# x1 kept in the output tensor, and the batch norm's results added to it by accumulating transfers

## The reference

```python
h = jnp.maximum(_layernorm(x, axis=-1), 0.0)
x = x + _L0_gnn_ref(h, adj, adj, Wq, Wk, Wv, Wo)      # 16-head attention with adj + adj as its bias
h = jnp.maximum(_layernorm(x, axis=-1), 0.0)
x = x + _L1_gnn_ref(h, adj, router_w, router_b, expert_w, bn_gamma, bn_beta)
...
scores = x.mean(axis=1) @ router_w + router_b
top1 = jnp.argmax(scores, axis=-1)
support = jnp.einsum('bnh,bhk->bnk', x, expert_w[top1])
out = jnp.einsum('bnm,bmk->bnk', adj, support)
# mean and variance of out over the rows of each expert's batches
y = (out - mean[top1]) * rsqrt(var[top1] + 1e-5) * bn_gamma[top1] + bn_beta[top1]
return relu(y)
```

## Time and profile before

| | us |
|---|---|
| median of 3 runs | 1561.91 (1559.69 to 1562.31) |
| the profiled execution | 1559.98 |
| its span | 1557.9 |
| PE busy in the span | 1480.9 (95%) |
| DVE busy | 1137.4 (73%) |
| ACT busy | 999.9 (64%) |
| POOL busy | 444.7 (29%) |

### The profile page before, as it was taken

The page is one execution under the profiler, slowest core; times in us unless marked ns, Lnnn a source line. Parts: engine busy times, 40 slices in busy tenths (PEclk is TensorE's granted clock), DMA queues, the critical chain, the costliest instruction groups (busy, mean ns, idle before and its releaser), DMA issues. The chain is left out here.

```text
span 1557.9 us, 39084 instructions
## 1 busy us (share of the span) xinstructions
PE 1480.9 (95%) x11474; PEld 1264.9 (81%) x11475; DVE 1137.4 (73%) x2641; ACT 999.9 (64%) x3145; POOL 444.7 (29%) x529
## 2 busy tenths in 40 slices
PE   7999999999999999999999999999969999998885
PEld 6888888888888888888888888888757777777775
DVE  4777777777777777777777777777676667676685
ACT  4667666766676677666666766676644454453495
POOL 0223222322223222222232222222223343443200
PEclk9999999999999999999999999999879999999997
DMA  5965556666655566665555666654524332220798
GB/s 180 254 145 142 125 125 144 150 151 152 144 131 125 128 148 147 155 148 145 126 125 135 148 150 151 149 139 112 136 89 135 123 124 87 67 68 14 268 406 327
DMA packets 142135, 230.37 MB, mean 148 GB/s; under 512 B 17666, under 2 KB 34050, under 8 KB 142082
## 3 DMA queue, kind: packets, MB, share of 16 engines
q1 hardware_dynamic: 133634, 212.95, 52.7%
q10 hardware_dynamic: 8448, 16.78, 2.8%
HBM read 89.15 MB, written 39.85 MB: 83 GB/s over the span
## 5 line engine op out<-in xcount | busy, mean ns | idle before, releaser
L268 POOL TENSOR_TENSOR prob<-prob,norm 128x512 f32<-128x512 f32 x256 | 266.3, 1040 | 789.3 <-DVE norm L372 789.3
L301 ACT ACTIVATE prob<-logits,neg_max 128x128 f32<-128x128 f32 x1024 | 398.1, 394 | 69.7 <-DVE neg_max L361 69.6
L43 PE MATMUL bank<-hT_hi,w_hi 128*128 128x256 f32 x1024 | 303.1, 296 | 2.5 <-DVE hT_lo L405 2.2
L43 PE MATMUL bank<-hT_lo,w_hi 128*128 128x256 f32 x1024 | 290.7, 284 | 0.0
L43 PE MATMUL bank<-hT_hi,w_lo 128*128 128x256 f32 x1024 | 290.6, 284 | 0.0
L356 DVE SCALAR_TENSOR_TENSOR logits<-scores_ps,adj 128x512 f32<-128x512 f32 x256 | 176.7, 690 | 134.1 <-PE scores_ps L420 133.6
L308 ACT ACTIVATE probT<-probT_ps 128x512 f32<-128x512 f32 x256 | 152.7, 596 | 143.2 <-PE probT_ps L427 143.2
L43 PEld LDWEIGHTS bank<-hT_hi,w_hi 128*128 128x128 f32 x1024 | 196.7, 192 | 21.2 <-issue 19.5
L43 PEld LDWEIGHTS bank<-hT_lo,w_hi 128*128 128x128 f32 x1024 | 197.3, 193 | 0.0
L43 PEld LDWEIGHTS bank<-hT_hi,w_lo 128*128 128x128 f32 x1024 | 196.9, 192 | 0.0
L301 ACT ACTIVATION_READ_ACCUMULATOR prob<-logits,neg_max 128x1 f32 x1024 | 195.7, 191 | 0.0
(11 more groups left out here) (138 smaller groups left out, 2921.5 us busy)
## 6 DMA issues: line engine op xcount, KB each, us to landing
stack<-qk SPq DMA_DIRECT2D x768, 128.0 KB, 2.5
x_in<-in_x SPq DMA_DIRECT2D x32, 512.0 KB, 4.7
x_res<-in_x SPq DMA_DIRECT2D x64, 256.0 KB, 2.9
x_dram<-x_res SPq DMA_DIRECT2D x64, 256.0 KB, 3.0
x_in<-x_dram SPq DMA_DIRECT2D x32, 512.0 KB, 3.7
y<-outs ACTq DMA_DIRECT2D x16, 1024.0 KB, 11.8
w_hi<-x_dram SPq DMA_DIRECT2D x8, 1024.0 KB, 17.9
out_dram<-outs SPq DMA_DIRECT2D x24, 256.0 KB, 2.0
```

The lines of the kernel that those rows point to most:

```text
L43: last = nc.tensor.matmul(out, a, b, start=(n == 0), stop=(n == len(terms) - 1))
L268: nc.gpsimd.tensor_tensor(prob[:, slot], prob[:, slot], norm[:, slot].unsqueeze(2).to_broadcast([N, R, N]), ALU.mult).then_inc(normed, 1)
L301: last = nc.scalar.activation(prob[:, slot, r], logits[:, slot, r], ACT.Exp, bias=neg_max[:, slot, r:r + 1], accum_out=row_sum[:, slot, r: ...
```

## The change

The attention writes x1 into y, the output tensor, instead of a tensor of its own, and the first pass of the expert layer reads it from there. In the last stage x1 isn't loaded any more. DVE writes max(., 0) alone, with one input instead of two. POOL issues, for each chunk, a transfer from SBUF to y with accumulation, which adds the chunk to the x1 that stands there. ACT issues no stores. SP issues only the loads of `out`, and waits for the same semaphores as before for them (y_stored now counts the accumulating transfers). Before the first transfer POOL waits until all loads of x1 in the first pass are done.

```diff
--- before.py
+++ after.py
@@ -542,9 +542,6 @@
 
     assert KC == G
 
-    x1_places = ([ew_hi[:, e].bitcast(F32) for e in range(E)] + [ew_lo[:, e].bitcast(F32) for e in range(E)]
-                 + [h2[:], x1_in[:]] + [z[:].bitcast(F32).rearrange("p g c n -> p g (c n)") for z in (z_hi, z_lo)])
-    X1_PLACES = len(x1_places)
     affine = sums[:, 0].rearrange("p a (c n) -> p a c n", c=KC)
 
     adjT_ps = ps("adjT_ps", [N, G, N])
@@ -567,7 +564,6 @@
         sem, ("var_all_ready", "inv_std_ready", "coef_ready", "rows_made"))
     t_made, act_applied, dve_applied, back_made, y_ready = map(
         sem, ("t_made", "act_applied", "dve_applied", "back_made", "y_ready"))
-    x1_chunk_loaded = [sem(f"x1_chunk_loaded{q}") for q in range(GROUPS)]
     out_chunk_loaded = [sem(f"out_chunk_loaded{q}") for q in range(STORED)]
     y_stored = [sem(f"y_stored{q}") for q in range(GROUPS)]
 
@@ -616,7 +612,6 @@
 
 
     ORDER = [*range(STORED, GROUPS), *range(STORED)]
-    LAST = ORDER.index(GROUPS - 1)
 
     def place_of(q):
 
@@ -666,10 +661,6 @@
             run(sp, body)
 
 
-            def load_x1(q):
-                if q != LAST:
-                    sp.dma_start(x1_places[q % X1_PLACES], x1_dram[G * ORDER[q]:G * ORDER[q] + G].rearrange("g n f -> n g f")).then_inc(x1_chunk_loaded[q], 16)
-
             def load_out(q):
                 sp.wait_ge(y_stored[q - STAYED], 16)
                 sp.dma_start(place_of(q), out_dram[G * ORDER[q]:G * ORDER[q] + G].rearrange("g n f -> n g f")).then_inc(out_chunk_loaded[q - STAYED], 16)
@@ -677,12 +668,7 @@
             sp.wait_ge(out_made, B)
             for g in range(G):
                 sp.wait_ge(out_stored[g], 16 * STORED)
-            for q in range(X1_PLACES):
-                load_x1(q)
             for q in range(STAYED, GROUPS):
-                if q + 2 < GROUPS:
-                    sp.wait_ge(y_ready, G * (q + 2 - X1_PLACES + 1))
-                    load_x1(q + 2)
                 load_out(q)
             for stored in y_stored:
                 sp.wait_ge(stored, 16)
@@ -723,6 +709,12 @@
             pool.wait_ge(var_all_ready, 1)
             nc.gpsimd.tensor_tensor(inv_std[:].rearrange("p e c -> p (e c)"), var[:].rearrange("p e c -> p (e c)"),
                                     minus_half[:], ALU.pow).then_inc(inv_std_ready, 1)
+            for half in range(2):
+                pool.wait_ge(x1_loaded[half], 16 * GROUPS)
+            for q in range(GROUPS):
+                pool.wait_ge(y_ready, G * (q + 1))
+                pool.dma_start(y[G * ORDER[q]:G * ORDER[q] + G].rearrange("g n f -> n g f"), place_of(q),
+                               accum_op=ALU.add).then_inc(y_stored[q], 16)
 
         @block.scalar
         def _(act):
@@ -754,10 +746,6 @@
             run(act, body)
             act.wait_ge(coef_ready, 1)
 
-            def store_y(q):
-                act.wait_ge(y_ready, G * (q + 1))
-                act.dma_start(y[G * ORDER[q]:G * ORDER[q] + G].rearrange("g n f -> n g f"), place_of(q)).then_inc(y_stored[q], 16)
-
             for k in range(B):
                 e = act.value_load(top1[0:1, G * ORDER[k // G] + k % G:G * ORDER[k // G] + k % G + 1], min_val=0, max_val=E - 1)
                 act.wait_ge(t_made, k + 1)
@@ -766,9 +754,6 @@
                     last = nc.scalar.activation(affine[:, k % AFFINE_RING, c], t_ps(k)[:, N * c:N * c + N], ACT.Relu,
                                                 bias=coef[:, 1, bass.ds(e, 1), c], scale=coef[:, 0, bass.ds(e, 1), c])
                 last.then_inc(act_applied, 1)
-                if k % G == G - 1 and k > G:
-                    store_y(k // G - 1)
-            store_y(GROUPS - 1)
 
         @block.vector
         def _(dve):
@@ -893,11 +878,7 @@
                     m = k - LAG
                     q, g = m // G, m % G
                     dve.wait_ge(back_made, m + 1)
-                    if g == 0 and q != LAST:
-                        dve.wait_ge(x1_chunk_loaded[q], 16)
-                    nc.vector.scalar_tensor_tensor(out=place_of(q)[:, g], in0=back_ps(m), scalar=0.0,
-                                                   in1=x1_places[q % X1_PLACES][:, g], op0=ALU.max,
-                                                   op1=ALU.add).then_inc(y_ready, 1)
+                    nc.vector.tensor_scalar(place_of(q)[:, g], back_ps(m), 0.0, None, ALU.max).then_inc(y_ready, 1)
 
         @block.tensor
         def _(pe):
@@ -988,7 +969,7 @@
 
 def program(nc, x, adj, wq, wk, wv, wo, router_w, router_b, expert_w, gamma, beta, y):
     B, N, D = x.shape
-    x1_dram = nc.dram_tensor("x1_dram", [B, N, D], F32, kind="Internal").ap()
+    x1_dram = y
     out_dram = nc.dram_tensor("out_dram", [B, N, D], F32, kind="Internal").ap()
     with ExitStack() as outer:
         def sem(name):
```

## The result

The changed kernel takes 1580.63 us (median of 4 runs, 1578.64 to 1581.49), the kernel before 1561.11 beside it: a ratio of 1.0124, with a 95% interval of 1.0106 to 1.0141. It is slower by 19.5 us; 1576.4 was forecast. The profiled execution has a span of 1578.1 us, against 1557.9.

The account below looks back on a forecast made before the run. The prediction took the DMA engines' ceiling to bound the last stage. Start at 1472.5, plus 82.9 for accumulates, 15.5 for loads of `out`, 1.5 to end and 4.0 offset gave 1576.4 us; own range 1568 to 1589, wide range 1555 to 1621.

Parts of the forecast that it names:

- The direction and the mechanism: Last stage: slower (chance 0.71), as DMA work of 98.4 us, no less than 95.8 before, starts only at 1472.5 us.
- the empty stretches up to 1472: Sign in the last stage: no DMA from 1452 to 1471 us, leaving some 20 us of full-rate time unused.
- the landings that grow: Sign: accumulating transfers' issue-to-landing times grow from chunk to chunk if their work exceeds 4.75 us a chunk.
- the 200 GB/s of the tail: Sign: rate in bytes near 200 GB/s while only accumulating transfers run, if a read of the destination isn't counted.
- the loads of `out`: Last stage: the sixth load lands by about 1522 us, chunk 15 is needed at about 1535, so no stall.
- The price of an accumulate, f = 2: Last stage: f is an accumulating transfer's cost in plain 1 MiB transfers of 2.59 us; taken as 2, or 5.18 us.
- Rival A: SBUF side is the limit: an accumulate costs 1 to 1.5 plain transfers; faster, device time 1546 to 1555.7 us; chance 0.24.
- Rival B: An accumulate costs 2.3 to 3 or more plain transfers, or POOL's issue exceeds 5.2 us; up to 1617.8 us; chance 0.29.
- the sum: Last stage: DMA starts at 1472.5 us, works 98.4 us, ends 1.5 us later: span 1572.4 us.
- the runs' offset: Added to the span for device time: 2.1 us around it plus 1.9 to the runs' median, 4.0 us.
- my 1.2 us: Last stage: time allowed from a chunk being ready to the first bytes of POOL's transfer, 1.2 us.
- The compute: Last stage: a chunk becomes ready each 4.75 us without stalls, so the compute ends near 1542 us.

Follow-up runs that it names:

- early4: Changed kernel, but x1 of the first 4 chunks loaded early, added by DVE and stored plainly; the other 12 accumulated: 1572.62 us, ratio 1.0071 to the kernel before.
- after_packed: Changed kernel with four batches' expert indices packed into one word, one register load a chunk on ACT and DVE: 1579.68 us, ratio 1.012 to the kernel before.
- late_loads: Kernel before, but SP waits for ACT's third batch of the last stage before its first load of x1: 1579.94 us, ratio 1.0127.
- add_in_sbuf: Changed kernel, but x1 is accumulated from y onto the chunk in SBUF, then stored by a plain transfer, both from POOL: 1622.16 us, ratio 1.0391 to the kernel before.
- plain_on_pool: Changed kernel, but POOL's 16 transfers are plain stores and x1 isn't added to y: 1559.54 us, ratio 0.9992 to the kernel before.
- plain_no_index: Changed kernel with plain POOL stores, x1 left out, and expert 0's coefficients used without index loads on ACT and DVE: 1541.44 us, ratio 0.9879 to the kernel before.
- before_pool_stores: Kernel before, with its 16 stores issued by POOL as soon as a chunk is ready instead of by ACT: 1561.04 us, ratio 0.9998.
- before_packed_pool: Kernel before, with expert indices packed four to a word and its stores issued by POOL: 1560.48 us, ratio 0.9998.

## Why the prediction was right, point by point

**The direction and the mechanism held.** The DMA work didn't shrink, it only moved to where it can't start early; the stretches of the changed kernel, early4 (less late work, 8.0 us back) and after_packed (faster compute gives nothing) each show it, and late_loads shows that the kernel before had no slack for a late start either. Of the signs that the prediction named, the empty stretches up to 1472, the landings that grow (9.4 us the shortest, 30.9 the median, 35.0 the longest) and the 200 GB/s of the tail came. The one that didn't is below, under the loads of `out`.

**The price of an accumulate, f = 2,** was the step on which all hung. Measured: 5.07 us in the tail (f = 1.96), and 93.1 us of engine time for 16, against 45.3 for 16 plain stores from the same queue (2.06). The work in the engines was taken at 82.9 us; at the share of 1.12 that the full stretches show, 93.1 is 83.1. The Trainium skill's rule (Collectives: The Full Stack, The bandwidth ceiling) has the adding transfer limited by its two source reads, with 1.93. The trace agrees with the price (1.96); it doesn't show that the reads are the limit.

**Rival A is out.** An accumulate doesn't cost one transfer, though x1 never enters SBUF. By the other rule of the Trainium skill (DMA: Bandwidth & Descriptors, Where 436 GB/s comes from) the SBUF ports are the limit; for an adding transfer no run here bears that out: the one of the changed kernel, whose chunk crosses once, takes 5.07 us, and the one of add_in_sbuf, whose sum is written into SBUF, 4.96. That the limit is the engines' reads fits all rows, but no run varied the reads alone: it is argued, not shown.

**Rival B is out:** 5.07 us and no more, and POOL is busy 1.28 us for an issue, less than a third of a chunk's time.

**What was off, 4.2 us in the time.** The span came 5.7 us over the sum, and the runs' offset 1.5 under it. Of the 5.7, the first bytes came later than my 1.2 us after the chunk was ready: in the stretch from 1472 to 1476 a share of 0.44 is 1.6 us of full work (4 x 0.44/1.12), so DMA began at 1474.4, not 1472.5 (1.9 us; POOL's first issue alone takes 1.50). From there the engines were full until about 1574.9 (4 x 0.82/1.12 = 2.9 us in the stretch from 1572), 100.5 us where the sum had 98.4 (2.1). And from the end of the full work to the end of the span it took 3.2 us, not 1.5 (1.7). The tail's price is 5.07, and the whole is yet some 4 us longer than 16 x 5.07 + 15.5 = 96.6. About 1 us of that is the start (the stretch from 1472 moved 0.12 MB in its 1.6 us of full work); the rest lies before the tail, and no run takes it apart. The 106 us that the prediction counts from 1451.0 to 1557.9 are 106.9; nothing hangs on it.

**The loads of `out` came later than the sum had them.** The sum took a transfer and a load in turn, 7.8 us a pair, so that the sixth load would have landed by 1522. But a load waits until the transfer out of its place has landed, and that transfer stands behind a backlog that grows. The transfer of chunk 5 was issued at 1497.75 and took 23.92 us, the sixth load behind it 13.07 more, and PE waited for it, where no wait was forecast (the chain that ends last, and PE's instruction):

```profile
1497.75 23.92 DMA y<-outs
1521.69 13.07 DMA outs<-out_dram
...
1534.80 1.12 PE L958 MATMUL z_ps<-ident,outs 128*128 128x128 f32 x4 [1.94 <-DMA outs<-out_dram]
```

It cost nothing, because the backlog of transfers was longer still.

**The compute** ended as the sum had it (1542.7 for 1542), but by errors that cancel, which is luck. A chunk took 4.29 us instead of 4.75, worth 6.9 us over 15 chunks. A slow spell from 1476 to 1485, not foreseen, took back 3.8 us of that (16.6 us for the first three chunks instead of 12.9), and the wait for `out` and what follows it some 2.5 (11.05 us for the last two instead of 8.58). The prediction had put a faster pace down to ACT's 16 issues (0 to 5.9 us). No run isolates them: with the stores on POOL the register loads slow down too and a chunk takes 4.88 us, and with packed indices and ACT's stores kept it takes 4.27. In the sum all this cost nothing, as the DMA queue stayed full.

## What to carry to other kernels

Don't price a transfer that adds by the bytes of its chunk: here it cost the DMA engines as much as a load and a store, so it freed SBUF and took an input off DVE, but saved no DMA time. (DVE's instruction was no faster for it: a median of 681 ns, as before.) Where DMA is the limit, the time at which work can start counts as much as its amount; loads that run ahead of the compute are worth more than transfers that can only follow it. Its one good place here was at the very end, for the chunks whose loads would stand in a queue ahead of something urgent. And where a place is reloaded after a transfer has left it, count the whole queue ahead of that transfer, not its own price alone.

## What the runs showed of the hardware

A register load from SBUF (TENSOR_LOAD, about 0.28 us in many stretches of these runs) takes up to 1.7 us in others in which chunks are stored, and where one is needed for each batch it becomes the pace: 5.39 against 4.19 us a chunk between plain_on_pool and plain_no_index. In the changed kernel nearly the whole slow spell goes with it (in after_packed the first three chunks take 13.3 us instead of 16.6); ACT's loads from 1474 to 1486 us:

```profile
L750 ACTq TENSOR_LOAD <-top x7: 284/1088/1338, 1474.2 to 1484.9; - x7
```

The queue of the stores has a part in it, by one execution of each kernel: before_pool_stores moves the same chunks as the kernel before, and only its stores go by POOL's queue (in 4352 packets instead of 8448). The median is 0.47 us there, and 0.29 with ACT's stores (lines under its experiment). But it isn't POOL's queue alone: the kernel before shows slow loads too, once its loads are done and only ACT's stores run (1540 to 1550 us):

```profile
L762 ACTq TENSOR_LOAD <-top x8: 273/405/874, 1539.8 to 1549.2; - x8
```

Nor is it any full DMA: in the changed kernel DMA is full from 1488 us on too, with more accumulates queued, and nine chunks pass at 4.29 us. What tells the conditions apart stays open. One load for four batches instead of four takes most of it out of the pace: a chunk then takes 4.27 us instead of 4.75 in the kernel before (ACT's stores), and 4.2 in before_packed_pool.
